# Expert stage: the second softmax weight from a logistic function on ScalarE, and down products ordered by PSUM bank

## The reference

```python
h = tok(x)                       # two recurrences of 8 steps over shifted tokens, width 64
h = h + attn(layernorm(h))       # 8 heads, scores exp(-gamma * |q - k|^2), no softmax
# x = layernorm(h) is the input of the expert layer
gate_logits = x @ gate_w + gate_b                    # 16 experts
topk_vals, topk_idx = jax.lax.top_k(gate_logits, 2)
topk_w = jax.nn.softmax(topk_vals, axis=-1)          # two weights for each token
h1 = relu(einsum('bsh,ehf->bsef', x, w1) + b1)
expert_out = einsum('bsef,efh->bseh', h1, w2) + b2
moe = sum over the two experts of topk_w * expert_out
y = layernorm(x + moe) * gamma + beta
h = h + y
```

## Time and profile before

| | |
|---|---|
| median of 3 runs | 812.05 us (811.7 to 814.22) |
| the profiled execution | 811.11 us, its span 809.1 us |
| TensorE busy | 747.9 us, 92% of the span |
| VectorE busy | 635.3 us, 79% |
| ScalarE busy | 533.2 us, 66% |
| GpSimd busy | 464.4 us, 57% |
| chain that ended last | PE 75%, DVE 14%, issue 5%, POOL 2%, ACT 2% |

### The profile page before, as it was taken

How to read it: one execution, slowest core, us unless ns; L and a number is a source line. 1 busy time by engine, 2 the same in 40 slices (tenths; PEclk the granted TensorE clock), 3 DMA queues, 4 the chain that set the end, 5 groups by cost and what they waited for, 6 DMA issues and landing times.

```text
span 809.1 us, 16776 instructions
## 1 busy us (share of the span) xinstructions
PE 747.9 (92%) x5680; PEld 430.8 (53%) x5680; DVE 635.3 (79%) x1569; ACT 533.2 (66%) x1042; POOL 464.4 (57%) x628
## 2 busy tenths in 40 slices
PE   2999879999999999999999998899999999999993
PEld 1344456666666666666666665444444444444431
DVE  3676668788887888878888786689998999989872
ACT  1565678888888888888888887544554555445442
POOL 8740255545455454554545542266777777777876
PEclk9999979999999999999999999999999999999997
DMA  6400022111221112211122112000000000000000
GB/s 159 124 2 2 2 52 53 27 40 42 52 53 27 40 41 53 52 28 39 43 53 51 29 35 45 1 3 1 8 14 8 9 8 8 10 13 8 7 8 19
DMA packets 22860, 25.70 MB, mean 32 GB/s; under 512 B 12888, under 2 KB 21720, under 8 KB 22648
## 3 DMA queue, kind: packets, MB, share of 16 engines
q1 hardware_dynamic: 21608, 23.57, 12.5%
q10 hardware_dynamic: 1168, 1.07, 0.6%
HBM read 5.30 MB, written 2.43 MB: 10 GB/s over the span
## 4 chain that ended last, share of the span: by engine, by line
PE 75%; DVE 14%; issue 5%; POOL 2%; ACT 2%; ACTq 1%; DMA 1%; POOLq 0%; SPq 0%; DVEq 0%
PE bank L1071 14%; PE bank L1119 11%; PE bank L1095 9%; PE bank L1209 8%; PE bank L1186 7%; PE bank L1097 7%; PE bank L999 6%; DVE gated L910 4%; PE bank L1123 3%; PE bank L989 2%; DVE top L892 1%; PE bank L1234 1%; DVE lg L899 1%; DVE wtok L903 1%; DVE lg L883 1%
## 5 line engine op out<-in xcount | busy, mean ns | idle before, releaser
L780 DVE TENSOR_SCALAR prob<-prob,cap_hi,cap_lo 125x500 f32<-125x500 f32 x256 | 156.3, 638 | 50.8 <-ACT prob L540 48.7
L406 POOL TENSOR_TENSOR sq<-sq 125x256 f32<-125x256 f32 x128 | 97.7, 774 | 156.5 <-ACT sq L554 132.8
L540 ACT ACTIVATE prob<-bank 125x500 f32<-125x500 f32 x256 | 148.8, 591 | 39.3 <-PE bank L1097 37.4
L443 POOL TENSOR_TENSOR gated<-relu,wb 128x500 f32<-128x500 f32 x96 | 119.9, 1249 | 59.3 <-ACT relu L635 57.3
L1209 PE MATMUL bank<-gated,w_sb 64*64 64x500 f32 x1024 | 136.0, 587 | 4.8 <-issue 4.8
L1186 PE MATMUL bank<-cs,w_sb 64*64 64x500 f32 x1024 | 135.0, 580 | 2.2 <-DVE gated L910 2.0
L910 DVE SCALAR_TENSOR_TENSOR gated<-bank,nb,wb 128x500 f32<-128x500 f32 x160 | 115.3, 730 | 26.1 <-PE bank L1186 25.9
L635 ACT ACTIVATE relu<-bank,b_sb 128x500 f32<-128x500 f32 x96 | 64.7, 674 | 95.4 <-PE bank L1186 95.4
L1071 PE MATMUL bank<-prob,u 125*64 125x250 f32 x1024 | 124.7, 384 | 0.5 <-DVE prob L780 0.5
L1095 PE MATMUL bank<-m,s 128*125 128x500 f32 x256 | 111.0, 433 | 10.2 <-issue 7.0
L795 DVE TENSOR_TENSOR m<-bank,m 64x500 fp32r<-64x500 f32 x128 | 86.4, 675 | 27.6 <-ACT m L549 26.3
(11 more groups left out here) (168 smaller groups left out, 1318.8 us busy)
## 6 DMA issues: line engine op xcount, KB each, us to landing
m<-m SPq DMA_DIRECT2D x128, 125.0 KB, 2.3
out<-res SPq DMA_DIRECT2D x16, 125.0 KB
xa<-xparts SPq DMA_DIRECT2D x4, 281.2 KB
w_sb<-in_w SPq DMA_DIRECT2D x1, 1024.0 KB
xw<-xparts SPq DMA_DIRECT2D x4, 140.6 KB
w_sb<-in_w SPq DMA_DIRECT2D x1, 512.0 KB
m<-s SPq DMA_DIRECT2D x32, 15.6 KB
xparts<-x_part SPq DMA_DIRECT2D x1, 375.0 KB, 4.6
```

What stands on the lines that cost most here:

```text
L406: gp.tensor_tensor(sq2[q][:, :, :], sq[q][:, :, 0:D // 2], sq[q][:, :, D // 2:D], ALU.add)\
L443: gp.tensor_tensor(gated[g % 8][:, :], relu_sb[n % 3][:, :], wb[q % 2][:, :], ALU.mult).then_inc(c_gatep, 1)
L540: act.activation(prob[v % PROBS][:, :, c, :], bank[5 + n % 3][0:T, 0:C].rearrange("p (h l) -> p h l", h=2), ACT.Exp).then_inc(b_exp, 1)
L780: dve.tensor_scalar(part, part, cap_hi[0:T, h:h + 1], cap_lo[0:T, h:h + 1], ALU.min, ALU.max)\
```

## The change

For all pairs but the first, ScalarE computes both weights from d with the logistic function (`top[9]` of -d, `top[10]` of d) in slot 4, in place of the one exponential. The steps n = 13, 14 and 15 of VectorE are left out; n = 16 comes directly behind n = 12 after group 7, and takes over the wait for ScalarE; n = 17 moves from group 9 to group 8. `c_gate` counts 15 to a pair then, which `gate_count` works out. In `down`, the four matmuls are ordered bank by bank in every slot, and in slot 0 the wait for the copy of `bank[0]` stands ahead of the first two, the wait for the copy of `bank[1]` ahead of the last two.

```diff
+        def gate_count(p, n):
+            first = min(n, 13) + max(0, n - 16)
+            return n if p == 0 else GATE + (p - 1) * (GATE - 3) + first
...
                 if v == 4 and valid(p):
-                    act.wait_ge(c_gate, GATE * p + GATE_D)
-                    act.activation(top[:, 7, :], top[:, 6, :], ACT.Exp).then_inc(c_e, 1)
+                    act.wait_ge(c_gate, gate_count(p, GATE_D))
+                    if p == 0:
+                        act.activation(top[:, 7, :], top[:, 6, :], ACT.Exp).then_inc(c_e, 1)
+                    else:
+                        act.activation(top[:, 9, :], top[:, 6, :], ACT.Sigmoid, scale=-1.0)
+                        act.activation(top[:, 10, :], top[:, 6, :], ACT.Sigmoid).then_inc(c_e, 1)
...
+                if n == (13 if p == 0 else 16):
+                    dve.wait_ge(c_e, p + 1)
                 if n == 13:
-                    dve.wait_ge(c_e, p + 1)
                     done(dve.tensor_scalar(top[:, 8, :], top[:, 7, :], 1.0, None, ALU.add))
...
-            GATE_AT = {2: (0,), 3: (1, 2, 3), 4: (4, 5, 6), 5: (7, 8, 9), 6: (10, 11), 7: (12, 13, 14), 8: (15, 16),
-                       9: (17,)}
+            GATE_AT_0 = {2: (0,), 3: (1, 2, 3), 4: (4, 5, 6), 5: (7, 8, 9), 6: (10, 11), 7: (12, 13, 14), 8: (15, 16),
+                         9: (17,)}
+            GATE_AT = {2: (0,), 3: (1, 2, 3), 4: (4, 5, 6), 5: (7, 8, 9), 6: (10, 11), 7: (12, 16), 8: (17,)}
...
             def down(q, v):
-                if v == 0:
-                    wait(pe, c_yl, q)
-                    wait(pe, c_yh, q)
-                    if q == 0:
-                        pe.wait_ge(b_res, PAIRS)
+                if v == 0 and q == 0:
+                    pe.wait_ge(b_res, PAIRS)
                 for g in (2 * v, 2 * v + 1):
                     wait_gated(pe, q, g)
-                for g, cols in ((2 * v, LO), (2 * v + 1, HI)):
-                    for rows, y in ((LO, bank[0]), (HI, bank[1])):
+                for rows, y, copied in ((LO, bank[0], c_yl), (HI, bank[1], c_yh)):
+                    if v == 0:
+                        wait(pe, copied, q)
+                    for g, cols in ((2 * v, LO), (2 * v + 1, HI)):
                         last = pe.matmul(y[cols, 0:C], w2_sb[rows, g, :], gated[g % 8][rows, :],
                                          start=v == 0, stop=v == 7, skip_group_check=True)
```

More of the change, by code:

```diff
@@ L866, in gate_step @@
                 else:
-                    dve.wait_ge(c_gate, GATE * p + (n - 1 if n == GATE_D else n))
+                    dve.wait_ge(c_gate, gate_count(p, n - 1 if n == GATE_D else n))
                 if n == 0:
@@ L953, in group_c @@
                 if valid(p):
-                    for n in GATE_AT.get(g, ()):
+                    for n in (GATE_AT_0 if p == 0 else GATE_AT).get(g, ()):
                         gate_step(p, n)
@@ L1230, in weights_c @@
             def weights_c(p):
-                pe.wait_ge(c_gate, GATE * (p + 1))
+                pe.wait_ge(c_gate, gate_count(p, GATE))
                 wait(pe, c_wbs, p)
```

## The result

The changed kernel takes 804.52 us (median of 6 runs, 803.26 to 805.22) against 812.83 us (6 runs, 811.70 to 814.22) of the kernel before: a ratio of 0.9894, with a 95% interval of 0.9881 to 0.9908. It is faster, by 1.1%. The forecast was 805.4 us in a range of 802.5 to 811.6. The profiled execution took 804.49 us with a span of 802.7 us, 6.4 us less than before.

What follows compares the result with a forecast made beforehand. The prediction took TensorE, busy in 92% of the span, as the bound, so only its idle time counts: 6.1 (`wtok`) + 0.3 (pair 15) + 0.3 (down products) = 6.7 us, from 812.05 to 805.4 us, range 802.5 to 811.6.

Steps and rivals of the forecast that it cites:

- The wait for `wtok`: TensorE's transposes of `weights_c` wait for VectorE's `wtok`; 0.51 us would go in each of 12 steps, 6.1 us.
- The sign I had named: In pairs 3 to 14, slot 6 starts of lines 1186 and 1234 lie 0.98 us apart if right.
- The replay against GpSimd: VectorE's new order on GpSimd's unchanged times: n = 16's first half waits, second gets in, `wtok` done 651.2 to 651.35.
- The lock rival: GpSimd's instruction beats n = 16's second half, delaying fused group 8; gain only 0.9 us, 811.1 us; chance 0.16.
- ScalarE and the table: Two logistic activations hidden in ScalarE's idle time; one table load at pair 1 costs zero, bounds 0 to 1.3 us.
- The down products: Slot 0: `bank[0]` matmuls start 0.33 us earlier, `bank[1]`'s as before; 0.02 us for each of 14 pairs, 0.3 us.
- the rival that the prediction hung on it: Slot 0 down products: matmuls in written order fill the 0.33 us, gaining 4.6 instead of 0.3, 801 us; chance 0.12.
- Order in the other slots: Down products in the other 7 of 8 slots: only the matmul order changes, taken as 0.
- The slower rival: Neighbouring same-row matmuls in 128 down slots, up to 0.13 us each: 17 us in all, 822 us; chance 0.06.
- Pair 15: Transposes of `wtok` in pair 15: 0.3 us gained (0.2 to 0.5), with fused group 8 some 0.4 us earlier.
- The sum: All terms together: 6.1 + 0.3 + 0.3 = 6.7 us, from 812.05 to 805.4 us.

Runs made afterwards that it cites:

- the gate change alone: The changed kernel with `down` as before, so only the gate part of the change: 804.86 us against 812.50, ratio 0.9900.
- the run with the copies first: The changed kernel with ScalarE's two copies of the down sums ahead of the relu of group 4 instead of behind it: 818.45 us, ratio 1.0074.
- the run with the steps dropped and not moved: The gate part alone, n = 13 to 15 dropped, but n = 16 left behind group 8 and n = 17 at group 9: 808.13 us against 811.86.
- the run with the sum later: The changed kernel with ScalarE's down-sum copies ahead of group 4's relu and GpSimd's sum of them behind group 9's product: 803.31 us, ratio 0.9893.
- the run of the down products alone: The kernel before with only `down` taken from the changed kernel, gate as before: 811.10 us, ratio 0.9985.
- the run with one wait: The changed kernel, matmuls still bank by bank, but both copies waited for ahead of the first down product: 806.41 us, ratio 0.9924.

## Why the prediction was right, point by point

- **The wait for `wtok`: right.** 0.51 us in each of 12 steps, as measured between starts; the gate change alone shortens the step from 17.10 to 16.59 us. The idle time beside the row (0.44) would have been too little. The sign I had named, starts in slot 6 that lie 0.98 us apart, holds in the gate change alone; in the full change the first up product stands 1.30 us ahead of the transposes (648.40 and 649.70), because it runs on the quarters that lead (see the down products).
- **The replay against GpSimd: right for the change.** First half blocked (1.17 us), second half through (0.21 us), `wtok` at 649.05, which is 651.17 in the old step's times (2.12 us on, as the `cxn` transposes stand); 651.2 to 651.35 was forecast. The slack is 0.65 us (0.5 to 0.6 forecast). The lock rival didn't come true here, but the run with the copies first shows that it was real. The second half got in 0.06 us ahead of GpSimd's product (647.17 and 647.23), and there was some luck in it, for a replay is not that exact. In the run with the steps dropped and not moved, GpSimd's product is recorded 0.03 us ahead of the second half and holds it up for 1.30 us; in the run with the sum later it is recorded 0.01 us ahead and doesn't.
- **ScalarE and the table: right.** The load of pair 1 in the trace after:

```profile
527.98 0.58 ACT L604 ACTIVATE cs<-bank 128x500 f32<-128x500 f32 x1
528.57 1.28 ACT L637 ACT_TABLE_LOAD   x1
530.51 0.21 ACT L637 ACTIVATE top<-top 125x4 f32<-125x4 f32 x1 [0.66 <-DVE top L898]
```

It starts as soon as ScalarE is free, not when d is ready; 0.66 us of idle time are left behind it, and it cost nothing. The Trainium skill ("ScalarE: Activation LUTs", What ACT_TABLE_LOAD costs) adds a drain of about 1.38 us to the load. Here the load follows the activation ahead of it at once (527.98 + 0.58 = 528.56), and the next activation starts 0.66 us behind its end, released by VectorE: there is no room for 1.38 us on either side.
- **The down products: right mechanism, size off.** I took 0.02 us a pair, measured are 0.05 to 0.06. The rows of the profile after show the quarters apart: records of up products (line 1197) start at 645.05, while records of bias products (line 1206) issued before them still start at 645.20. The two quarters behind `bank[1]` start 0.36 us behind the other two (643.74, and 644.10 below), the first down slot takes 1.41 us instead of 1.07, and the lead is still 0.36 us in the next up products (645.05 and 645.41). I had expected no up product behind to start earlier; those on the leading quarters do, at 645.05, which is 647.17 in the old step's times, against 647.54 before. The rule of the Trainium skill ("TensorE: Matmul & The Clock Gate", The mechanism) that matmuls start in program order is contradicted by these rows too, and the rival that the prediction hung on it (4.6 us) is excluded by the run of the down products alone. Nor did that rival follow from the rule: it needs, beyond the order, that two quarters at work keep the other two from working.

  Where the 0.05 us come from can be read around the end of the copy of `bank[1]`:

```profile
643.47 0.57 ACT L631 ACTIVATE y_high<-bank 128x500 f32<-128x500 f32 x1
...
644.10 0.19 PEld L1219 LDWEIGHTS bank<-gated,w_sb 64*64 64x64 f32 x4 [0.17 <-ACT y_high L631]
```

  Before, the copy ended at 646.16 and the four matmuls began at 646.26, 0.10 us later. Now it ends at 644.04 and the two matmuls begin at 644.10 with their weight load, 0.06 us later. So 0.04 of the 0.05 us are a shorter way from the copy to the first start, a term that the prediction didn't have, and only about 0.01 is left for two starts at once instead of four. In the run with one wait the distance is 0.10 us again. A likely reason, which no run tests: in the kernel before and in that run, the waits for the two gated tiles stand between the wait for `y_high` and the first weight load; in the changed kernel they stand ahead of it.
- **Order in the other slots: zero, right.** The slower rival asked for 0.05 us a slot or more; the run with the bank order and one wait shows 0.00 in the step.
- **Pair 15: right.** 17.83 became 17.54 us, 0.29 against a forecast 0.3.
- **The sum.** 6.7 us forecast, 7.1 in the traces, of which 12 x 0.56 + 0.3 = 7.0 are named. The term mis-sized is the down products (0.7 instead of 0.3). The median moved by 8.3 to 8.4 us; I take the further 1.2 us to be scatter of the front part, which no trace shows. That 804.52 us lies only 0.9 us from the forecast, within its own range of 804 to 807, is in part luck: the gain was 1.6 us larger than forecast, and the forecast had started 0.8 us too low, from 812.05 us where the median of six runs is 812.83. The distance of the profiled execution to the median before, 0.94 us from three runs, was too small: from 17 runs it is 1.4.

## What to carry to other kernels

Read a wait from the distance of starts to a step that doesn't have it, and replay moved instructions one by one against the other engine that shares their path to memory; summed durations (1.86 us freed here) say little, and an early place pays only when the chain put there is short. Idle time that vanishes from a list is not yet time gained: when half of a job starts earlier and the other half sets the end, nothing moves. Compare step lengths, not medians, when the question is below the scatter between programs.

## What the runs showed of the hardware

- The quarters of TensorE's array start their matmuls independently of the order across quarters, and a lead of 0.36 us of two of them lasts until the next product over the full array: the up products of slot 6, just ahead of the transposes, are spread over 1.36 us (at 648.40) instead of 1.05.
- VectorE's small steps between tiles in SBUF and GpSimd's instructions hold each other up both ways and for whole instructions: a VectorE step of 0.22 us took up to 1.30 us, a GpSimd sum of 1.24 us took 1.70. The fused instruction (line 920), which reads PSUM and `wb`, isn't held up: it takes 0.73 us at 647.31, beside GpSimd's product of 647.23 to 648.50. The Trainium skill ("SBUF — State Buffer", Who interferes with whom) describes this as an exclusive lock for a VectorE instruction with two inputs in SBUF against a GpSimd instruction that reads SBUF, and for any VectorE instruction in a 2-port mode. These traces agree for lines 888, 908, 909 and 913, with two inputs each. Line 892 of the kernel before has one input and was held up too (1.11 us); in which mode it ran, no trace shows.
- The part ahead of the expert stage, with the same instructions, ended between 517.7 and 521.2 us in ten traces.
